# Two adaLN layers on one core: part of the convolution's front moved into the MLP before it

## The chip, the cores and the metric

The kernel runs on one core of a Trainium2 chip. The metric is the time of one execution on the device in microseconds (us). The engines: PE is TensorE (matmuls, and transposes by the identity), DVE is VectorE, ACT is ScalarE, POOL is GpSimd, SP is SyncE, which here only issues DMA.

## The reference

Input x has shape (2, 2048, 128). Layer 0 is a gated linear attention and then two blocks of windowed attention with a gated MLP; layer 1 is a causal convolution by softmaxed scores and a mixture of 16 experts. What matters here is the seam between them:

```python
# end of L0: second block's MLP
x = x + h @ w2 + b2                    # h = a * gelu(g), a, g from layernorm(shift_token(x)) @ w1 + b1
...
x = x + gb * _L0_ffn_ref(...)          # gate and residual of layer 0
# start of L1
h = _layernorm(x, axis=-1) * (1 + ca) + sa
x = x + ga * _L1_attn_ref(h, ...)
# _L1_attn_ref: 16 heads of 8
z = softmax(einsum('bse,he->bsh', x, W_A) * SCALING, axis=1)     # over the 2048 positions
v = einsum('bse,fe->bsf', x, W_V)
out[i] = sum over j <= i of z[i - j] * v[j]                        # per head
return out @ W_O.T + b_O
# then
h = _layernorm(x, axis=-1) * (1 + cb) + sb
x = x + gb * _L1_ffn_ref(h, ...)       # gate, top 2 of 16 experts, relu
```

## The kernel before

The 4096 rows are 32 tiles of 128 rows, 16 per batch element; they stay in SBUF as `x_rows`, and what layer 0's second half makes is in `y_rows`. Four tiles form a group, so there are eight groups. Each stage is a block with one hand-written program per engine; engines meet only through semaphores inside a block, and all of them meet at a barrier between blocks.

**The layers' block** (`layers_in_one_block`, L1436) runs attention, MLP, attention, MLP. The order of an engine's work is set by `Phase` (L164): a list of stages, each a function with a lag, and step s calls every stage for group s minus its lag, in the order of the list. For the MLP (`gated_mlp`, L1238) the lists are: TensorE `up` (lag 2, three gate and three up products), `turn` (1), `down` (3); VectorE `residual` (4, adds the down product to `y_rows`), `statistics` (0), `multiply` (2, three products), `normalize` (0); ScalarE `gelu` (2, three) and `hn_columns` (1); GpSimd `inverse_std` (0). `between` holds calls that are made ahead of a step. A phase of the second MLP has steps 0 to 11.

**The convolution's block** (`convolution_and_experts`, L1850) comes next. Its front is, per group: GpSimd gates y (`gated`, L1951), VectorE adds it to x and takes layer-norm statistics (`statistics`, L1981 to L1991), GpSimd raises to the power of minus a half (`inverse_std`, L1957), VectorE makes offsets (L1996), ScalarE normalizes four tiles into `cv_rows` (`normalized`, L2199), TensorE turns them (`turn_h`, L2092), ScalarE copies the columns to `cv_hT` with scale and shift (`h_columns`, L2207), TensorE projects to scores z (L2100) and values v (L2109), and ScalarE evicts both (`outputs`, L2215 and L2218). VectorE takes a maximum per group (`group_max`, L2002). When a batch element's four groups are in, ScalarE takes the exponential of 16 x 2048 scores (`z_exp`, L2224) and VectorE normalizes them (`probabilities`, L2017). SyncE then writes them to DRAM (L1939) and fetches them back as Toeplitz tiles `cv_toep` (L1932), 32 blocks wide in three parts, for each of eight convolution steps. There is one such buffer: the next step's part is fetched when the matmuls have used it (`p_used`).

Behind the front stands the experts' set-up (`experts`, L1492): ten rounds, in each of which TensorE fills a PSUM bank (`prepare`: rounds 0 to 3 transpose four weight tiles each, 4 and 5 make the gate, 6 to 9 are the first batch element's products) and ScalarE (even rounds) or VectorE (odd rounds) evicts it (`take`, L1736 and L1615). `set_bank` names the bank, and a round waits until the bank's last one has been evicted:

```python
set_bank = lambda r: bk[r % 2 + (2 if r < ROUNDS_BEFORE else 0)]     # L1543
...
set_done(pe, r - 2)                                                   # L1785
```

Then TensorE runs the convolution (`convolve`, L2124), which waits for `vnow` from ScalarE (L2233), with the experts' phases behind and between. GpSimd meanwhile adds the output bias to x (L1970).

## Time and profile before

| | us |
|---|---|
| three runs, median (lowest to highest) | 1212.86 (1210.7 to 1214.95) |
| the profiled execution's own time | 1215.1 |
| its span in the profile | 1213.3 |
| TensorE busy in the span | 1068.4 (88%) |
| VectorE, ScalarE, GpSimd busy | 879.7, 818.5, 661.1 |
| mean granted TensorE clock | 0.955 |

The span is the time from the first to the last instruction in the profile. "Busy" counts the time in which an engine executes something. The granted clock is the share of TensorE's full 2.4 GHz clock; it has two levels, 1.0 and 0.5. Lines named L... are those of the kernel before; the changed kernel has other numbers.

### The profile page before, as it was taken

The page shows a single profiled execution, that of the slowest core. Times are in us where ns is not written, and L with a number is a line of the kernel's source. Part 1 is how long each engine was busy: PE and PEld are TensorE (multiplying, and loading weights), DVE is VectorE, ACT ScalarE, POOL GpSimd, SP SyncE. Part 2 cuts the span into 40 slices and gives each one's busy share as a digit, 9 for nine tenths or more (in the row PEclk, how much of TensorE's full clock was granted, in tenths as well). Part 3 has the DMA queues.
Part 4 walks back from the last instruction along what each step waited for, and adds up shares of the span by engine and source line. Part 5 has one row for each costly group of instructions (what it writes and reads, how often), then busy time and mean ns, then how long its engine had stood idle before and what let it go on. Part 6 is the DMA issues. An engine that isn't in the chain of part 4 may idle for free. (4 is left out here: it accounts for less than half of the span.)

```text
span 1213.3 us, 33822 instructions
## 1 busy us (share of the span) xinstructions
PE 1068.4 (88%) x11683; PEld 733.6 (60%) x11683; DVE 879.7 (73%) x2948; ACT 818.5 (67%) x2658; POOL 661.1 (54%) x1070
## 2 busy tenths in 40 slices
PE   6699994799999998798899999997996778799996
PEld 4467673377777776465577777775663577654442
DVE  4799997588888886374788888885547312079998
ACT  3688883588888887323888988884327403178886
POOL 1578995788888886111888888882106300002222
PEclk9899997799999998989999999998997899899998
DMA  7000000112222121311112111111001486600000
GB/s 232 2 2 11 11 2 1 27 45 55 57 52 54 45 46 45 117 32 34 41 44 47 45 44 45 45 45 27 1 1 44 92 194 137 142 5 16 16 18 18
DMA packets 69566, 58.79 MB, mean 48 GB/s; under 512 B 42262, under 2 KB 53442, under 8 KB 69122
## 3 DMA queue, kind: packets, MB, share of 16 engines
q1 hardware_dynamic: 69411, 56.83, 19.3%
q8 instruction: 84, 1.38, 0.5%
q14 instruction: 71, 0.58, 0.2%
HBM read 29.40 MB, written 2.38 MB: 26 GB/s over the span
## 5 line engine op out<-in xcount | busy, mean ns | idle before, releaser
L1168 PE MATMUL psum<-wa_wqkv,wa_hT 128*128 128x512 f32 x384 | 189.8, 603 | 4.4 <-DVE wa_tmp L1032 3.2
L1124 ACT ACTIVATE wa_p<-psum,wa_nb 128x128 f32<-128x128 f32 x512 | 183.7, 398 | 4.3 <-DVE wa_nb L1048 4.2
L1048 DVE CUSTOM_DVE_ANT_0 psum<-psum,wa_bias 128x128 f32<-128x128 f32 x512 | 133.0, 323 | 51.2 <-PE psum L1197 51.2
L1014 POOL TENSOR_TENSOR wa_p<-wa_p,wa_rrs 128x512 f32<-128x512 f32 x128 | 133.2, 1040 | 47.7 <-DVE wa_rrs L1057 47.7
L1594 POOL TENSOR_TENSOR ex_total<-ex_total,mod 128x128 f32<-128x128 f32 x32 | 15.5, 485 | 218.3 <-DVE ex_total L1722 218.3
L1124 ACT ACTIVATION_READ_ACCUMULATOR wa_p<-psum,wa_nb 128x1 f32 x512 | 122.2, 239 | 0.0
L1840 PE MATMUL psum<-ex_wc,ex_hT 128*128 128x512 f32 x256 | 117.6, 602 | 3.4 <-DVE ex_yw L1705 2.2
L1769 ACT ACTIVATE ex_yw<-psum,ex_w 128x128 f32<-128x128 f32 x384 | 106.7, 400 | 20.1 <-DVE ex_w L1698 7.4
L985 POOL TENSOR_TENSOR wa_qr<-wa_qr,wa_tmp 128x512 f32<-128x512 f32 x64 | 81.8, 1278 | 64.3 <-DVE wa_tmp L1032 64.3
L1134 ACT ACTIVATE wa_pT<-psum 128x512 f32<-128x512 f32 x128 | 76.6, 598 | 39.7 <-PE psum L1177 39.7
L1381 ACT ACTIVATE ml_gelu<-psum,ml_b 128x512 f32<-128x512 f32 (+1 forms) x48 | 32.9, 685 | 85.0 <-PE psum L1408 71.6
L1177 PE MATMUL psum<-ident,wa_p 128*128 128x128 f32 x512 | 81.0, 282 | 9.5 <-ACT wa_kT L1117 3.2
L1032 DVE TENSOR_TENSOR wa_tmp<-psum,wa_tabs 128x512 f32<-128x512 f32 x128 | 87.2, 681 | 0.0
L1168 PEld LDWEIGHTS psum<-wa_wqkv,wa_hT 128*128 128x128 f32 x384 | 64.3, 195 | 37.9 <-issue 32.9
L1840 PEld LDWEIGHTS psum<-ex_wc,ex_hT 128*128 128x128 f32 x256 | 45.2, 189 | 65.8 <-issue 65.0
L990 POOL TENSOR_TENSOR wa_kr<-wa_kr,wa_tmp 128x512 f32<-128x512 f32 x64 | 81.5, 1273 | 2.2 <-DVE wa_tmp L1032 2.2
L2124 PE MATMUL psum<-cv_v_now,cv_toep 64*64 64x256 f32 (+31 forms) x2048 | 67.8, 290 | 15.1 <-DMA cv_toep<-cv_zpad 7.6
L1220 PE MATMUL psum<-wa_wo,wa_oT 128*128 128x128 f32 x512 | 70.8, 283 | 11.1 <-DVE wa_oT L1063 11.1
L1722 DVE TENSOR_TENSOR ex_yw<-ex_yw 128x1024 f32<-128x1024 f32 (+2 forms) x96 | 78.4, 816 | 1.7 <-ACT ex_yw L1769 0.8
L1039 DVE TENSOR_REDUCE wa_ss<-wa_sq 128x16 f32<-128x1024 f32 x64 | 77.4, 1210 | 1.6 <-ACT wa_sq L1095 1.5
L2124 PEld LDWEIGHTS psum<-cv_v_now,cv_toep 64*64 64x64 f32 x2048 | 62.6, 142 | 21.0 <-issue 17.9
L1048 DVE DVE_READ_ACCUMULATOR2_ANT wa_nb<- 128x1 f32 x512 | 72.5, 142 | 0.0
(256 smaller groups left out, 2978.2 us busy)
## 6 DMA issues: line engine op xcount, KB each, us to landing
wa_vm<-wa_v SPq DMA_DIRECT2D x127, 128.0 KB, 2.3
cv_toep<-cv_zpad SPq DMA_DIRECT2D x32, 256.0 KB, 4.5
cv_toep<-cv_zpad SPq DMA_DIRECT2D x16, 512.0 KB, 6.9
wa_tabs<-in_rotations_dram SPq DMA_DIRECT2D x2, 2048.0 KB, 8.2
wa_rows<-y_rows SPq DMA_DIRECT2D x31, 128.0 KB
wa_rows<-y_rows SPq DMA_DIRECT2D x31, 127.0 KB
x_rows<-in_L_attn_x_dram SPq DMA_DIRECT2D x4, 512.0 KB, 6.0
out_dram<-x_rows SPq DMA_DIRECT2D x32, 64.0 KB, 1.5
```

The source lines that it names most:

```text
L985: nc.gpsimd.tensor_tensor(q, q, tmp[:, t % 2, 0, :], ALU.add).then_inc(g_q.sem, 1)
L990: nc.gpsimd.tensor_tensor(k, k, tmp[:, t % 2, 1, :], ALU.add).then_inc(g_k.sem, 1)
L1014: nc.gpsimd.tensor_tensor(p, p, cols_bc(rrs[:, t % 2, r, :], P), ALU.mult)\
L1032: nc.vector.tensor_tensor(halves(heads(cross)), halves(src)[:, :, ::-1, :], halves(rows_bc(sin, WH)), ALU.mult).then_inc(done.sem, 1)
L1048: m = nc.vector.tensor_tensor_reduce(out=s, in0=s, in1=edges, scale=-1.0, scalar=MAX_FLOAT, op0=ALU.add, op1=ALU.min, accum_out=nb[:, t % ...
L1124: e = nc.scalar.activation(pr[:, t % 2, r, h, :], sim_bank[r][:, P * h:P * h + P], ACT.Exp, bias=nb[:, t % 2, r, h:h + 1], scale=-1.0, acc ...
L1168: nc.tensor.matmul(bank, hT[:, t % 3, :], wqkv[:, INNER * k:INNER * k + INNER], start=True, stop=True).then_inc(done.sem, 1)
L1177: m = nc.tensor.transpose(turn_bank[:, P * k:P * k + P], src(t, k), c.ident[:, :])
L1722: nc.vector.tensor_tensor(to, y[:, 0:n, :], y[:, n:2 * n, :], ALU.add).then_inc(v_half[k].sem, 1)
L1769: m = nc.scalar.activation(yw[:, t % 2, e, :], up_banks[(4 * t + k) % 6][:, P * j:P * j + P], ACT.Relu, scale=w[:, t // GT % 2, t % GT, e: ...
L1840: nc.tensor.matmul(up_banks[number % 6], hT[:, t // GT % 3, t % GT, :], wc[:, batch(t), chunk(k)], start=True, stop=True).then_inc(p_up[k] ...
L2124: mm = nc.tensor.matmul(conv_bank[a][side(k), CD * lag:CD * BLOCKS] .rearrange("p (n d) -> p n d", d=CD), toep[side(a), k, HALF * lag:HALF ...
```

## The change

- A class `ConvolutionRows` holds the front's tiles and its functions `gated`, `statistics`, `inverse_std`, `offsets`, `normalized`, and the turning of the convolution's weights. Its constant `IN_MLP` is 5.
- In the second MLP these functions run for groups 0 to 4, each in its engine's phase with a lag of 5 (4 for the gate). The weights are loaded by SyncE behind its staging, turned by TensorE after the last down projection, and copied by ScalarE after a table load.
- In the convolution's block only groups 5 to 7 remain. GpSimd gates all three, then takes the three powers; VectorE does all statistics, then all offsets, then the weights and the mixing matrix, and only then the maxima. ScalarE normalizes into `y_rows` in place of a ring `cv_rows`, and does not wait for the turn before it.
- ScalarE's first exponential stands behind the outputs of group 3, where it stood behind those of group 5.
- The ten set-up rounds go over six banks in place of two.
- A group's four `bn_aggr` no longer have a wait and a no-op before each.

```diff
+class ConvolutionRows:
+    IN_MLP = TILES // 4 - 3
...
+    def gated(self, gp, g):
+        c, t = self.c, self.tiles(self.y, g)
+        b = 4 * g // NT
+        c.nc.gpsimd.tensor_tensor(t, t, rows_bc(c.mod[:, 0, b, GB, :], 4), ALU.mult).then_inc(self.g_gated.sem, 1)
...
+    def statistics(self, dve, g):
+        nc, x = self.c.nc, self.c.x
+        self.g_gated.wait(dve, g)
+        t = self.tiles(x, g)
+        nc.vector.tensor_tensor(t, t, self.tiles(self.y, g), ALU.add).then_inc(self.v_x.sem, 1)
...
+    def normalized(self, act, g):
+        self.v_shift.wait(act, g)
+        for t in range(4 * g, 4 * g + 4):
+            m = self.c.nc.scalar.activation(self.y[:, t, :], self.c.x[:, t, :], ACT.Identity,
+                                            scale=self.rstd[:, t:t + 1], bias=self.shift[:, t:t + 1])
+        m.then_inc(self.a_norm.sem, 1)
...
+        def conv_rows(eng, do, lag):
+            def f(g):
+                if g - first < conv.IN_MLP:
+                    do(eng, g - first)
+            return [] if more else [(f, lag)]
...
-            return Phase([(inverse_std, 0)], first, GROUPS)
+            return Phase(conv_rows(gp, conv.inverse_std, 5) + [(inverse_std, 0)] +
+                         ([] if more else [(conv_gated, 4)]), first, GROUPS)
...
-            return Phase([(residual, 4), (statistics, 0), (multiply, 2), (normalize, 0)], first, GROUPS,
+            return Phase([(residual, 4)] + conv_rows(dve, conv.statistics, 5) +
+                         [(statistics, 0), (multiply, 2), (normalize, 0)] + conv_rows(dve, conv.offsets, 5), first, GROUPS,
...
+            if not more:
+                between[10] = lambda: nc.scalar.preload_act_table_set("natural_log_exp_and_others")
+                between[11] = lambda: conv.copy_weights(act, turn_bank)
+            return Phase([(gelu, 2), (hn_columns, 1)] + conv_rows(act, conv.normalized, 5), first, GROUPS,
...
+            return Phase([(up, 2), (turn, 1), (down, 3)], first, GROUPS, begin=lambda: wait_layer(pe, l),
+                         between=None if more else {11: conv_weights})
...
-    set_bank = lambda r: bk[r % 2 + (2 if r < ROUNDS_BEFORE else 0)]
+    set_bank = lambda r: bk[2 + (r + 4) % 6 if r < ROUNDS_BEFORE else r % 2]
+    SET_BANKS = 6
...
-                set_done(pe, r - 2)
+                set_done(pe, r - (SET_BANKS if r < ROUNDS_BEFORE else 2))
...
-                for g in range(GROUPS + 2):
-                    if g < GROUPS:
-                        normalized(g)
+                for g in range(1, GROUPS + 2):
+                    if conv.IN_MLP <= g + 1 < GROUPS:
+                        conv.normalized(act, g + 1)
...
-                    if g == PER_B + 3:
+                    if g == PER_B + 1:
                         z_exp(0)
```

VectorE in a middle step of the second MLP, before (names that begin with ml_ are the MLP's, with wa_ the attention's, with cv_ the convolution's):

```order
L1355 TENSOR_TENSOR y_rows<-y_rows,psum 128x512 [waits ml_p_down]
L1327 BN_STATS ml_st<-wa_rows 128x6 [waits wa_rows_in3] x4
L1331 BN_AGGR ml_mv<-ml_st 128x2 [waits ml_v_bn_mv]
L1348 SCALAR_TENSOR_TENSOR ml_mT<-psum,ml_b,ml_gelu 128x512 [waits ml_p_up,ml_a_gelu,ml_p_down]
L1348 SCALAR_TENSOR_TENSOR ml_mT<-psum,ml_b,ml_gelu 128x512 [waits ml_p_up,ml_a_gelu]
L1348 SCALAR_TENSOR_TENSOR ml_mT<-psum,ml_b,ml_gelu 85x512 [waits ml_p_up,ml_a_gelu]
L1338 TENSOR_SCALAR ml_hn<-wa_rows,ml_mv,ml_rstd 128x128 [waits ml_p_hn,ml_g_eps_rstd]
```

and the same step in the changed kernel:

```order
L1460 TENSOR_TENSOR y_rows<-y_rows,psum 128x512 [waits ml_p_down]
L1300 TENSOR_TENSOR x_rows<-x_rows,y_rows 128x512 [waits cv_g_gated]
L1303 BN_STATS cv_st<-x_rows 128x6 [waits cv_v_x_stat]
L1307 BN_AGGR cv_mv<-cv_st 128x2 [waits cv_v_x_stat]
L1311 TENSOR_SCALAR cv_mv<-cv_mv 128x4 [waits cv_v_x_stat]
L1432 BN_STATS ml_st<-wa_rows 128x6 [waits wa_rows_in3] x4
L1436 BN_AGGR ml_mv<-ml_st 128x2 [waits ml_v_bn_mv]
L1453 SCALAR_TENSOR_TENSOR ml_mT<-psum,ml_b,ml_gelu 128x512 [waits ml_p_up,ml_a_gelu,ml_p_down]
L1453 SCALAR_TENSOR_TENSOR ml_mT<-psum,ml_b,ml_gelu 128x512 [waits ml_p_up,ml_a_gelu]
L1453 SCALAR_TENSOR_TENSOR ml_mT<-psum,ml_b,ml_gelu 85x512 [waits ml_p_up,ml_a_gelu]
L1443 TENSOR_SCALAR ml_hn<-wa_rows,ml_mv,ml_rstd 128x128 [waits ml_p_hn,ml_g_eps_rstd]
L1316 SCALAR_TENSOR_TENSOR cv_shift<-cv_mv,cv_rstd 128x4 [waits cv_g_rstd]
```

Four operations came in ahead of the MLP's own statistics, and the offset behind its normalization.

ScalarE in the front of the convolution's block, changed kernel, around the first exponential (L1323 is `normalized`, L2261 `h_columns`, L2269 and L2272 `outputs`, L2278 `z_exp`):

```order
L2261 ACTIVATE cv_hT<-psum,mod_cols 128x512 [waits cv_p_v,cv_p_h]
L2269 ACTIVATE cv_z<-psum 16x512 [waits cv_p_z]
L2272 ACTIVATE cv_v<-psum 128x512 [waits cv_p_v]
L2278 ACTIVATE cv_z,cv_zsum<-cv_z,cv_zneg 16x2048 [waits cv_v_zneg]
L1323 ACTIVATE y_rows<-x_rows,cv_shift,cv_rstd 128x128 [waits cv_v_shift]
L1323 ACTIVATE y_rows<-x_rows,cv_shift,cv_rstd 128x128 x3
L2261 ACTIVATE cv_hT<-psum,mod_cols 128x512 [waits cv_p_v,cv_p_h]
```

Here the exponential stands between the outputs of group 3 and the normalized rows of group 7; before, it stood behind the last normalized rows and the outputs of group 5, with the columns of group 7 after it.

TensorE in the experts' set-up, before and then changed:

```order
L1789 MATMUL psum<-ident,ex_w_in 128x128 [waits ex_loaded,cv_a_v]
L1789 MATMUL psum<-ident,ex_w_in 128x128 x7
L1789 MATMUL psum<-ident,ex_w_in 128x128 [waits ex_a_set]
L1789 MATMUL psum<-ident,ex_w_in 128x128 x3
L1789 MATMUL psum<-ident,ex_w_in 128x128 [waits ex_v_set]
L1791 MATMUL psum<-ident,ex_gate_in 128x16 [waits ex_a_set]
L1796 MATMUL psum<-ex_gateT,ex_mix 128x16 [waits ex_a_set,ex_v_mix,ex_v_set]
```

```order
L1905 MATMUL psum<-ident,ex_w_in 128x128 [waits ex_loaded,cv_a_v]
L1905 MATMUL psum<-ident,ex_w_in 128x128 x15
L1907 MATMUL psum<-ident,ex_gate_in 128x16
L1912 MATMUL psum<-ex_gateT,ex_mix 128x16 [waits ex_a_set,ex_v_mix]
L1916 MATMUL psum<-ex_wT,ex_mix 128x512 [waits ex_a_set]
```

The sixteen transposes and the gate's transpose wait for no eviction of a set-up bank any more.

## Rows read from the trace of the kernel before

**Rows 1.** Stages: busy us (count) per engine, granted clock, DMA share, GB/s
```profile
855.29:908.42 53.13, 52.25 (x262) 33.55 (x260) 26.78 (x73) 16.22 (x23) 5.00 (x8) 1.00 0.00 1
909.42:948.61 39.19, 24.82 (x307) 14.26 (x307) 27.40 (x103) 29.69 (x63) 20.19 (x19) 0.83 0.16 38
948.61:963.53 14.92, 9.28 (x29) 4.99 (x30) 8.15 (x15) 5.15 (x10) 10.80 (x8) 0.77 0.61 141
963.53:1060.00 96.47, 79.28 (x2229) 72.91 (x2230) 14.11 (x51) 17.15 (x44) 0.00 (x0) 0.93 0.68 154
```

**Rows 2.** Timeline, TensorE, second MLP: start, us, line, operation, [idle before <-releaser]
```profile
863.56 1.02 PE L1408 MATMUL psum<-ml_hnT,ml_w 128*128 128x512 f32 x2
...
871.83 1.02 PE L1408 MATMUL psum<-ml_hnT,ml_w 128*128 128x512 f32 x2
```

**Rows 3.** Timeline, VectorE, end of that MLP step
```profile
868.98 0.75 DVE L1348 SCALAR_TENSOR_TENSOR ml_mT<-psum,ml_b,ml_gelu 85x512 f32<-85x512 f32 x1 [0.97 <-PE psum L1412]
869.65 1.10 DVE L1338 TENSOR_SCALAR ml_hn<-wa_rows,ml_mv,ml_rstd 128x128 f32<-128x128 f32 x4
```

**Rows 4.** Timeline, ScalarE, first GELU of the next step
```profile
872.89 0.69 ACT L1381 ACTIVATE ml_gelu<-psum,ml_b 128x512 f32<-128x512 f32 x1 [2.76 <-PE psum L1408]
```

**Rows 5.** Timeline, VectorE, front of the convolution's block and second softmax
```profile
910.87 1.74 DVE L1981 TENSOR_TENSOR x_rows<-x_rows,y_rows 128x512 f32<-128x512 f32 x1 [1.73 <-POOL y_rows L1951]
912.65 0.87 DVE L1984 BATCH_NORM_STATS2 cv_st<-x_rows 128x6 f32<-128x128 f32 x4
913.44 0.37 DVE L1988 BATCH_NORM_AGGREGATE cv_mv<-cv_st 128x2 f32<-128x6 f32 x4
...
916.63 0.15 DVE L1996 SCALAR_TENSOR_TENSOR cv_shift<-cv_mv,cv_rstd 128x4 f32<-128x4 f32 x1
916.73 0.69 DVE L1981 TENSOR_TENSOR x_rows<-x_rows,y_rows 128x512 f32<-128x512 f32 x1
...
944.80 1.27 DVE L2017 TENSOR_SCALAR cv_z<-cv_z,cv_zrec 16x2048 f32<-16x2048 f32 x1
946.00 1.26 DVE L2002 TENSOR_REDUCE cv_zpart<-cv_z 16x1 f32<-16x512 f32 x2
...
952.09 2.05 DVE L2017 TENSOR_SCALAR cv_z<-cv_z,cv_zrec 16x2048 f32<-16x2048 f32 x1
```

**Rows 6.** Timeline, GpSimd, first two gates and the bias additions
```profile
909.59 2.47 POOL L1951 TENSOR_TENSOR y_rows<-y_rows,mod 128x512 f32<-128x512 f32 x2
...
949.35 10.80 POOL L1970 TENSOR_TENSOR x_rows<-x_rows,cv_bog 128x512 f32<-128x512 f32 x8 [12.81 <-DVE cv_bog L2025]
```

**Rows 7.** Timeline, ScalarE, front of the convolution's block and set-up
```profile
916.82 1.65 ACT L2199 ACTIVATE cv_rows<-x_rows,cv_shift,cv_rstd 128x128 f32<-128x128 f32 x4 [3.64 <-DVE cv_shift L1996]
...
921.20 0.76 ACT L2207 ACTIVATE cv_hT<-psum,mod_cols 128x512 f32<-128x512 f32 x1
...
948.61 2.01 ACT L2224 ACTIVATE cv_z<-cv_z,cv_zneg 16x2048 f32<-16x2048 f32 x1
...
950.61 0.57 ACT L1736 ACTIVATE ex_wT<-psum 128x512 f32<-128x512 f32 x1
```

**Rows 8.** Timeline, TensorE, front of the convolution's block and set-up
```profile
912.02 0.33 PE L2153 MATMUL psum<-ident,cv_w_in 128*128 128x128 f32 x1 [3.61 <-DMA cv_w_in<-in_L_attn_W_A_dram]
...
918.52 1.11 PE L2092 MATMUL psum<-ident,cv_rows 128*128 128x128 f32 x4 [5.90 <-ACT cv_rows L2199]
...
924.22 1.98 PE L2109 MATMUL psum<-cv_wvT,cv_hT 128*64 128x64 f32 x32
...
930.60 1.15 PE L2109 MATMUL psum<-cv_wvT,cv_hT 128*64 128x64 f32 x32
...
954.80 1.12 PE L1789 MATMUL psum<-ident,ex_w_in 128*128 128x128 f32 x4 [2.91 <-DVE ex_wT L1615]
...
957.57 5.32 PE L1800 MATMUL psum<-ex_wT,ex_mix 128*128 128x512 f32 x8
```

**Rows 9.** Window of one us, TensorE busy, granted clock, DMA share, GB/s
```profile
912.00:913.00 1.00, 0.60 (x3) 0.86 0.28 55
```

More of the change, by code:

```diff
@@ L1240, in gated_mlp @@
+def gated_mlp(c, y, given, ctx, conv):
     nc, inp, bk = c.nc, c.inp, c.bank
@@ L1306, in sync @@
                     given.stage(sp, "attention", l + 1, GT * g, GT)
+            else:
+                conv.load(sp)
         def gpsimd(gp):
@@ L1317, in inverse_std, with conv_gated @@
                   .then_inc(g_rstd.sem, 1)
-            return Phase([(inverse_std, 0)], first, GROUPS)
+            def conv_gated(g):
+                v_y.wait(gp, g)
+                if g - first < conv.IN_MLP:
+                    conv.gated(gp, g - first)
+            return Phase(conv_rows(gp, conv.inverse_std, 5) + [(inverse_std, 0)] +
+                         ([] if more else [(conv_gated, 4)]), first, GROUPS)
         def vector(dve):
@@ L1424, in down, with conv_weights @@
                 m.then_inc(p_down.sem, 1)
-            return Phase([(up, 2), (turn, 1), (down, 3)], first, GROUPS, begin=lambda: wait_layer(pe, l))
+            def conv_weights():
+                a_hn.wait(pe, last)
+                conv.turn_weights(pe, turn_bank)
+            return Phase([(up, 2), (turn, 1), (down, 3)], first, GROUPS, begin=lambda: wait_layer(pe, l),
+                         between=None if more else {11: conv_weights})
         readers = {turn_at: a_hn, down_at: v_y}
@@ L1947, in _ @@
                 nc.gpsimd.memset(zeros[:, :], 0.0).then_inc(g_zero, 1)
-                def gated(g):
-                    t = tiles_of(y, g)
-                    nc.gpsimd.tensor_tensor(t, t, rows_bc(c.mod[:, 0, batch(g), GB, :], GT), ALU.mult)\
-                      .then_inc(g_gated, 1)
-                def inverse_std(g):
-                    gp.wait_ge(v_eps, g + 1)
-                    t = slice(GT * g, GT * g + GT)
-                    nc.gpsimd.tensor_tensor(rstd[:, t], mv[:, t, 1], c.minus_half[:, 0:GT], ALU.pow)\
-                      .then_inc(g_rstd, 1)
-                for g in range(GROUPS + 1):
-                    if g < GROUPS:
-                        gated(g)
-                    if g >= 1:
-                        inverse_std(g - 1)
+                late = range(conv.IN_MLP, GROUPS)
+                for g in late:
+                    conv.gated(gp, g)
+                for g in late:
+                    conv.inverse_std(gp, g)
                 on_gpsimd.fill(gp)
@@ L1967, in _ @@
                 for g in range(GROUPS):
-                    gp.wait_ge(a_norm, GT * g + GT)
+                    conv.a_norm.wait(gp, g)
                     t = tiles_of(c.x, g)
@@ L2042, in _ @@
                 dve.sem_inc(v_conv, 1)
-                for g in range(GROUPS + 4):
-                    if g < GROUPS:
-                        statistics(g)
-                    if 1 <= g <= GROUPS:
-                        offsets(g - 1)
-                    if g >= 4:
-                        group_max(g - 4)
-                    if g == PER_B + 4:
-                        probabilities(0)
+                late = range(conv.IN_MLP, GROUPS)
+                for g in late:
+                    conv.statistics(dve, g)
+                for g in late:
+                    conv.offsets(dve, g)
                 weights()
                 on_vector.mixing(dve)
+                for g in range(GROUPS):
+                    group_max(g)
+                    if g == PER_B - 1:
+                        probabilities(0)
                 probabilities(1)
@@ L2192, in _ @@
             def _(act):
-                def normalized(g):
-                    act.wait_ge(v_shift, g + 1)
-                    if g >= 2:
-                        act.wait_ge(p_h, g - 1)
-                    for i in range(GT * g, GT * g + GT):
-                        nc.scalar.activation(rows[:, g % 2, i % GT, :], c.x[:, i, :], ACT.Identity,
-                                             scale=rstd[:, i:i + 1], bias=shift[:, i:i + 1]).then_inc(a_norm, 1)
                 def h_columns(g):
```

138 lines of the change are left out of this document (75 added, 63 removed).

## The prediction

> **What bounds the kernel now.** I read the busy times by stage first, because a share over the whole span hides which stage pays [rows 1]. The second MLP (855.29 to 908.42 us) has TensorE busy for 52.25 of 53.13 us at full clock, with VectorE at 26.78, ScalarE at 16.22 and GpSimd at 5.00: TensorE bounds it, and the others have room. The next stage, the convolution's front (909.42 to 948.61), has no full engine: TensorE 24.82 of 39.19, ScalarE 29.69, at a mean clock of 0.83. A chain is the bound there. Then come 14.92 us from the last value eviction to the convolution's first matmul (TensorE 9.28, clock 0.77), and eight convolution steps that take 96.47 us, or 12.1 us each. The change touches the first three. The rest should only start earlier.
>
> Next the timelines of the engines. One MLP step on TensorE starts at 863.56 and the next at 871.83, so a step is 8.27 us [rows 2]. VectorE does its last multiplication, which waits for TensorE, at 868.98, and its normalization at 869.65 to 870.75; it then has nothing to do until the next step's residual some 1.3 us later [rows 3]. ScalarE idles for 2.76 us before it starts the next GELU at 872.89 [rows 4]. In the front stage TensorE's first transposed rows come only at 918.52, having waited for ScalarE's normalized rows, which begin at 916.82 behind GpSimd and VectorE [rows 5 to 8].
>
> **The change, part by part.** *Five groups inside the MLP.* Each adds on VectorE an addition (0.7, as a residual), 0.87 + 0.37 for statistics, and two small operations of 0.15 = 2.25 us [rows 5]. A full MLP step holds the normalization's 1.10, three multiplications of 0.75, a residual of 0.7 and statistics of 1.2, or 5.3 us; the stage's mean is less (26.78 us in 6.4 steps, 4.2), since its last steps lack parts. 5.3 + 2.25 = 7.6 of 8.27: it fits. The new work stands ahead of the multiplications, which pushes the first two back by 2.1 us; the third waited for TensorE anyway (0.97 us) and stays where it is. GpSimd gets a gate of 1.25 [rows 6] and a power on top of the pair it has (5.00 us for four pairs, 1.25 each): at most 3.7 of 8.27. Its order is power of the convolution, power of the MLP, gate, so the gate runs when VectorE starts to normalize. What then happens the trace shows: the addition at 910.87, beside a gate, took 1.74 us where it takes 0.69 alone [rows 5]. I charge up to 1.25 us of such waiting a step. It falls on VectorE's idle 1.3 us at the step's end, which the displaced multiplications leave alone. ScalarE then does four normalized tiles in 1.65 us [rows 7], from about 871.5 to 873.2, in front of a GELU that would start at 872.89: 0.3 us late, and that GELU's product is wanted by a multiplication 2.1 us later than before. Cost to TensorE, which sets the end: nothing. If the cover goes, every us over 8.27 is paid five times. The weight loads (four DMAs) move to SyncE's queue behind its staging, over 50 us before their use: nothing. Their three transposes and three copies come behind the last down projection and move the end of the block by some 0.4 us (transposes 0.4, copies 0.6, beside a residual of 0.69 that stood there). The table load of 1.3 us falls into ScalarE's idle end.
>
> The Trainium skill ("SBUF — State Buffer", Who interferes with whom) says that the port pair which VectorE and GpSimd share is held exclusively for a whole instruction, by operations with two SBUF inputs or in a two-port mode. By it bn_stats pays nothing and the MLP step stays under 8.27 us, as in the sum; the 1.74 us agrees.
>
> *The front stage, 39.2 us before.* I follow the new order from about 909.9, where the block now starts.
> 1. TensorE turns group 0 at once, where it waited until 918.52 [rows 8]. At full clock a group costs it 24.82 x 0.83 / 8 = 2.6 us by its busy time and mean clock [rows 1]; I take 2.5, as some of that was set-up.
> 2. The three late groups: gate to 911.3, then VectorE's addition waits for the second gate as before (912.5), 3 x 2.1 us of statistics to 919.0, offset, and ScalarE normalizes group 5 at 919.1 to 920.8. ScalarE has that ahead of group 3's columns, so TensorE, done with groups 0 to 2 at 918.9, waits 3 us.
> 3. VectorE goes on with offsets to 920.3, weights 0.85, mixing some 3 us (it took the 2.7 between the first bias addition at 949.35 and the softmax at 952.09, and meets those additions again, 1.35 each [rows 5, 6]), four maxima of 0.63 and two small ones [rows 5], with starts and signals between: 927.3.
> 4. ScalarE has the first exponential, 2.0 us, at that point of its order, then normalization of group 7 (1.65) and columns of group 5 (0.76) [rows 7]: 931.6. TensorE has stood since about 928: over 4 us.
> 5. Three groups of 2.5 us and their evictions: 939.4 at full clock.
> That gives a stage end of 939.4 against 948.61, 9.2 us less. But TensorE's granted clock dropped to half (mean 0.86 in the slice) in the us after it had idled from 908.42 to 912.02 [rows 8, 9], and the same 32 matmuls took 1.98 us at half and 1.15 at full clock [rows 8]. The wait of step 4 is as long. Half clock over some 4.4 us of three groups' work costs 2.1 us. I take that: the stage ends at 941.5, **7.1 us less**. Bounds: 9.2 with no fall, and 5 if the clock stays low through the three groups.
>
> The Trainium skill ("TensorE: Matmul & The Clock Gate", HAM oscillation) warns against just such gaps between bursts; a kernel that obeyed it would be worth 9.2 here, and it gets 7.1. The row agrees that a gap of this size can do it.
>
> *From the last eviction to the convolution, 14.9 us before.* TensorE waited in the set-up for one bank after another, the worst time 2.91 us for VectorE's copy, which stood behind the second softmax; then its last eight passes took 5.32 us at mostly half clock [rows 8]. With six banks the sixteen transposes need no eviction. ScalarE: exponential 2.0, two copies of 0.57 [rows 7], a small one, so the gate round comes at +3.2 us. VectorE's normalization of the second softmax no longer meets the bias additions (the 2.05 at 952.09 become the 1.27 of 944.80 [rows 5]), and its copies of 0.7 come from +3.5 on, in time. Four rounds of 0.93 (the MLP's pairs of passes, six in the 5.2 us ahead of its down projection, take 0.86 each) bring TensorE to +7.1, the last copy to +7.8. 14.9 - 7.8 = **7.1 us less**. Bounds: 8 with nothing late, 4 if the rounds run at half clock.
>
> *Earlier softmax.* VectorE's result was ready at 946.07 [rows 5], and store and first fetch were in place by 963.53 at the latest, where TensorE started without a transfer to wait for: at most 17.5 us. Now it is ready at about 931.1, so all is in place by 948.6 at the latest, and the convolution starts at 949.3. Worth nothing by itself, needed so that nothing is lost. GpSimd's eight bias additions move from 949 to 921 on and are waited for by nobody then. Eight convolution steps depend on one Toeplitz buffer each, not on a clock on the wall: they move as they are.
>
> Sum: -7.1 - 7.1 = -14.2 us, with the late block end in it. The profiled execution has 1215.1 us for a span of 1213.3; the median of three is 1212.86, 2.2 less, and I take the difference from the median: **1198.7 us**.
>
> **The rivals.** *Clock stays full* through the softmax wait: -16.3, 1196.6. For it: a gap may be shorter than I draw. Against: 3.61 us were enough [rows 8, 9]. *Clock low for longer*, also after the wait of step 2 or in the set-up: 2 to 4 us more, 1200.7 to 1202.7. *VectorE becomes the MLP's bound*: its 7.6 us plus more waiting for GpSimd than its tail covers (the addition, the small addition after the statistics and the normalization, up to 1.25 each, make 7.6 + 2.5 = 10.1). 1 to 1.8 us over in five steps gives back 5 to 9 us: 1203.7 to 1207.7. For it: the 1.74 row. Against: GpSimd's operations start after the VectorE ones they wait for, so only one of three can meet. *Slower:* the same ring closes over ScalarE: GELU waits behind the normalized tiles, those for the offset, that for the power, that for the statistics, and the multiplication for GELU. It decides from a step of 8.27 + 14.2/5 = 11.1 us on; at 12 us the time is 1212.9 - 14.2 + 5 x 3.7 = 1217.2. Against it are the 2.76 us that ScalarE idles before each GELU [rows 4]. *The change does not do what it says:* the front gets shorter, but the convolution's steps, with DMA at 0.68 [rows 1] and waits for transfers, meet the clock at other points and give a good part back: 1206 to 1213.
>
> **How the numbers follow.** Forecast (1197.5 to 1200.5) 0.50; full clock 0.17; low clock longer 0.12; MLP bound by VectorE 0.11; gains given back 0.06, half of it within the limit; slower 0.04. The range 1195.0 to 1204.5 takes in the forecast, the clock cases, their unknown waits and the mild end of the MLP case, some 0.83. A measurement here tells about 0.3% (3.6 us) from no change: faster 0.93, same 0.03, slower 0.04.
>
> **What would show it.** Steps of 8.27 us still in the second MLP; the block change at about 909.9; transposed rows right behind it; ScalarE idle before the first exponential, which begins near 927; TensorE idle for about 4 us behind group 4 and at half clock after; the last value eviction near 941.5; the set-up's wait for VectorE gone and the first convolution matmul near 949.3; from there to the end the same time as before. Wrong would be an MLP step above 8.5 us, a first convolution matmul that waits for a transfer, or a convolution of more than 98 us.

## The result, and the profile after

| kernel | median, us | runs | lowest to highest | ratio to the kernel before (95%) |
|---|---|---|---|---|
| before, beside it | 1214.95 | 7 | 1210.70 to 1219.01 | 1 |
| with the change | 1200.61 | 7 | 1197.35 to 1207.50 | 0.9885 (0.9856 to 0.9915) |

The change takes 14.3 us off (1214.95 less 1200.61), or 1.15%. The profiled execution of the changed kernel has 1197.35 us for a span of 1195.5, the fastest of its seven. That of before has 1215.1 for 1213.3.

The stages of the changed kernel, in busy times: the MLP up to its last down projection, the front up to the last value eviction, the set-up of the mixing, and the eight convolution steps. They answer to [rows 1]; each column is a sum over the engine, with its number of instructions, and then the mean granted clock.

```profile
core 0: us, PE busy (x) PEld busy (x) DVE busy (x) ACT busy (x) POOL busy (x), PEclk, DMA share, GB/s
856.73:909.86 53.13, 52.26 (x264) 33.72 (x262) 38.08 (x128) 25.30 (x44) 16.28 (x18) 1.00 0.00 1
911.15:942.59 31.44, 24.06 (x304) 14.13 (x304) 19.81 (x55) 21.37 (x39) 18.14 (x17) 0.89 0.34 82
942.59:950.79 8.20, 6.25 (x30) 3.78 (x30) 4.10 (x7) 4.91 (x9) 0.00 (x0) 1.00 0.48 100
950.79:1041.23 90.44, 72.86 (x2209) 67.74 (x2210) 13.16 (x48) 16.78 (x43) 0.00 (x0) 1.00 0.72 165
```

The MLP takes 53.13 us as before, although VectorE now works 38.08 us in it (26.78 before) and GpSimd 16.28 (5.00). The front went from 39.19 to 31.44 us and the set-up from 14.92 to 8.20. The block starts 1.29 us behind the last down projection (911.15 less 909.86), where it was 1.00. That is -7.75 - 6.72 + 0.29 = **-14.2 us**, the forecast's sum.

The two profiled spans differ by more, 17.8 us, and this is what the other stages add. The second MLP starts 1.4 us later in this execution (856.73 against 855.29); what stands before it is the same in both kernels. The eight convolution steps take 90.44 us against 95.42 (963.53 to 1058.95; the last window of [rows 1] runs 1.05 us past them): the clock was full through all of them (1.00 above). A second profile of the same changed kernel, below, gives 95.92 at 0.93. So those 5 us are the luck of one execution, and the medians' 14.3 is the number to keep. It agrees with the 14.2 of the stages.

Now the MLP's steps in detail. TensorE's down projections, one group to a line (the start, the duration, engine, line, operation, tiles, shapes and count):

```profile
862.31 2.84 PE L1532 MATMUL psum<-ml_w,ml_mT 128*128 128x128 f32 x24
870.58 2.84 PE L1532 MATMUL psum<-ml_w,ml_mT 128*128 128x128 f32 x24
878.85 2.84 PE L1532 MATMUL psum<-ml_w,ml_mT 128*128 128x128 f32 x24
```

They stand 8.27 us apart, as in [rows 2]. VectorE's timeline of that step, with the idle time before an operation and what ended it in brackets, GpSimd's beside it, and ScalarE's two rows at its end:

```profile
865.19 0.69 DVE L1460 TENSOR_TENSOR y_rows<-y_rows,psum 128x512 f32<-128x512 f32 x1 [1.27 <-PE psum L1532]
...
869.11 2.05 DVE L1453 SCALAR_TENSOR_TENSOR ml_mT<-psum,ml_b,ml_gelu 128x512 f32<-128x512 f32 x3
871.08 1.64 DVE L1443 TENSOR_SCALAR ml_hn<-wa_rows,ml_mv,ml_rstd 128x128 f32<-128x128 f32 x4
872.65 0.15 DVE L1316 SCALAR_TENSOR_TENSOR cv_shift<-cv_mv,cv_rstd 128x4 f32<-128x4 f32 x1
873.46 0.69 DVE L1460 TENSOR_TENSOR y_rows<-y_rows,psum 128x512 f32<-128x512 f32 x1 [0.67 <-PE psum L1532]
```
```profile
869.59 1.03 POOL L1415 TENSOR_TENSOR ml_rstd<-ml_mv,minus_half 128x4 f32<-128x4 f32 x1
870.60 1.26 POOL L1288 TENSOR_TENSOR y_rows<-y_rows,mod 128x512 f32<-128x512 f32 x1
```
```profile
872.83 1.65 ACT L1323 ACTIVATE y_rows<-x_rows,cv_shift,cv_rstd 128x128 f32<-128x128 f32 x4 [1.27 <-DVE cv_shift L1316]
874.38 0.67 ACT L1487 ACTIVATE ml_gelu<-psum,ml_b 128x512 f32<-128x512 f32 x1
```

VectorE's step is 873.46 - 865.19 = 8.27 us, and 0.67 us of it are still idle. The normalization takes 1.64 us instead of 1.10 [rows 3], since GpSimd's gate runs at 870.60 to 871.86. ScalarE's GELU has lost the idle time of [rows 4] to the normalized tiles and comes directly behind them. Its place in the step has hardly moved: it starts 0.92 us behind the residual (874.38 less 873.46), where it was 0.86 (872.89 less the residual at 872.03 in the trace of before).

The front on TensorE, from its first transposed rows on (this answers to [rows 8]):

```profile
911.19 1.06 PE L2159 MATMUL psum<-ident,y_rows 128*128 128x128 f32 x8 [0.96 <-PEq L1583]
...
919.99 0.66 PE L2159 MATMUL psum<-ident,y_rows 128*128 128x128 f32 x4
924.38 1.86 PE L2167 MATMUL psum<-cv_hT,cv_waT 128*16 128x512 f32 x2 [3.73 <-ACT cv_z L2269]
926.18 1.78 PE L2176 MATMUL psum<-cv_wvT,cv_hT 128*64 128x64 f32 x32
...
933.70 1.18 PE L2167 MATMUL psum<-cv_hT,cv_waT 128*16 128x512 f32 x2 [2.52 <-ACT cv_z L2269]
934.80 1.98 PE L2176 MATMUL psum<-cv_wvT,cv_hT 128*64 128x64 f32 x32
```

There are **two** waits, and the granted clock falls after each. The first, 3.73 us, stands ahead of group 3's projection: ScalarE copies group 3's columns only after it has normalized group 5. The second, 2.52 us, stands ahead of group 5's projection, behind the first exponential. At half clock the two score matmuls behind the first wait take 1.86 us where they take 1.03 at full clock, and the 32 value matmuls behind the two waits take 1.78 and 1.98 instead of 1.15. The first wait begins here, on GpSimd and VectorE (this answers to [rows 5, 6]):

```profile
911.32 3.72 POOL L1288 TENSOR_TENSOR y_rows<-y_rows,mod 128x512 f32<-128x512 f32 x3
```
```profile
912.61 2.98 DVE L1300 TENSOR_TENSOR x_rows<-x_rows,y_rows 128x512 f32<-128x512 f32 x1 [2.04 <-POOL y_rows L1288]
```

VectorE's first addition is issued when the first gate is done and ends 0.55 us after the third is (915.59 and 915.04): 2.98 us for an operation of 0.69. Group 5 is then normalized at 921.45 (ScalarE), 10.3 us behind the block's start.

The set-up, which in [rows 8] waited for one bank after another:

```profile
942.64 1.97 PE L1905 MATMUL psum<-ident,ex_w_in 128*128 128x128 f32 x16 [0.70 <-ACT cv_v L2272]
...
945.84 0.59 PE L1912 MATMUL psum<-ex_gateT,ex_mix 128*128 128x16 f32 x4 [1.07 <-ACT ex_gateT L1852]
946.27 3.68 PE L1916 MATMUL psum<-ex_wT,ex_mix 128*128 128x512 f32 x8
950.79 1.49 PE L2191 MATMUL psum<-cv_v_now,cv_toep 64*64 64x256 f32 x24 [0.83 <-ACT cv_v_now L2287]
```

All sixteen transposes run in one piece, the last eight passes are at full clock (3.68 us for 5.32 before), and the convolution starts without a transfer to wait for.

### The profile page after: what moved, and what is told of

The parts are those of the page before. It is cut to its first block and busy times, and to the rows that moved or that the text cites. A ratio compares the mean times of both kernels' runs of the same rounds, so it can differ in the third digit from the quotient of the medians.

```text
span 1195.5 us, 33784 instructions
## 1 busy us (share of the span) xinstructions
PE 1059.4 (89%) x11683; PEld 728.9 (61%) x11683; DVE 879.8 (74%) x2948; ACT 820.7 (69%) x2658; POOL 659.8 (55%) x1070
## 3 DMA queue, kind: packets, MB, share of 16 engines
q8 instruction: 84, 1.38, 0.5%
## 5 line engine op out<-in xcount | busy, mean ns | idle before, releaser
L1177 PE MATMUL psum<-ident,wa_p 128*128 128x128 f32 x512 | 80.8, 281 | 10.1 <-ACT wa_kT L1117 3.2
L2191 PE MATMUL psum<-cv_v_now,cv_toep 64*64 64x256 f32 (+31 forms) x2048 | 63.9, 279 | 15.4 <-DMA cv_toep<-cv_zpad 7.9
L1220 PEld LDWEIGHTS psum<-wa_wo,wa_oT 128*128 128x128 f32 x512 | 64.9, 199 | 12.1 <-DVE wa_oT L1063 12.1
```

What stands on the lines that cost most here:

```text
L1177: m = nc.tensor.transpose(turn_bank[:, P * k:P * k + P], src(t, k), c.ident[:, :])
L1220: m = nc.tensor.matmul(hw_bank[:, 0:E], oT[:, t % 2, k, :], wo[:, k, :], start=k == 0, stop=k == PAIRS - 1)
```

## The experiments

Theory A is the forecast's: the front and the banks each give about 7 us, the early exponential gives nothing but keeps the transfers ahead, and the waits in the front cost a fall of the clock. The rivals say that one part carries the whole gain, that the early exponential costs time, or that VectorE in the MLP is near its limit. Twelve kernels were run in three sets, each set beside its own runs of the kernel before (medians 1216.96, 1216.85 and 1215.79). The ratio of *triple_stats* rests on two runs, the others on four to ten. The stages below are from one profiled execution each, in us. "Delay" is from the last down projection's end to the block's first instruction. The last column is the sum of the three to its left, the one to compare, since it leaves out what happened upstream and in the convolution. Among the variants of the changed kernel the intervals of the ratios overlap, so most differences between them are shown by the stages alone; that the stages repeat, *after_again* shows.

| kernel | median | ratio (95%) | delay | front | set-up | sum |
|---|---|---|---|---|---|---|
| before | 1214.95 | 1 | 1.00 | 39.19 | 14.92 | 55.1 |
| changed | 1200.61 | 0.9885 (0.9856 to 0.9915) | 1.29 | 31.44 | 8.20 | 40.9 |
| two_banks | 1204.59 | 0.9904 (0.9874 to 0.9934) | 1.30 | 31.50 | 14.16 | 47.0 |
| late_softmax | 1197.72 | 0.9851 (0.9811 to 0.9890) | 1.29 | 29.11 | 8.43 | 38.8 |
| mlp_alone | 1205.73 | 0.9904 (0.9871 to 0.9937) | 1.30 | 29.11 | 13.78 | 44.2 |
| six_alone | 1209.23 | 0.9960 (0.9936 to 0.9984) | 1.00 | 39.22 | 9.93 | 50.2 |
| fill | 1200.10 | 0.9869 (0.9831 to 0.9908) | 1.30 | 29.97 | 8.20 | 39.5 |
| gates | 1201.07 | 0.9863 (0.9845 to 0.9882) | 1.21 | 29.04 | 8.20 | 38.5 |
| in6 | 1198.64 | 0.9852 (0.9828 to 0.9875) | 2.68 | 28.10 | 8.19 | 39.0 |
| triple_stats | 1203.32 | 0.9882 (0.9860 to 0.9904) | 1.30 | 31.45 | 8.20 | 41.0 |
| after_again | 1200.97 | 0.9870 (0.9836 to 0.9905) | 1.30 | 31.44 | 8.20 | 40.9 |
| best1 | 1194.92 | 0.9831 (0.9799 to 0.9863) | 3.73 | 25.39 | 8.43 | 37.6 |
| conv_fill | 1202.03 | 0.9886 (0.9859 to 0.9914) | 1.30 | 31.44 | 8.21 | 41.0 |
| best1_fill | 1198.85 | 0.9857 (0.9828 to 0.9886) | 3.74 | 26.25 | 8.43 | 38.4 |

**The parts of the change, undone or alone.** *two_banks* is the changed kernel with its set-up on two banks:

```diff
-    set_bank = lambda r: bk[2 + (r + 4) % 6 if r < ROUNDS_BEFORE else r % 2]
-    SET_BANKS = 6
+    set_bank = lambda r: bk[r % 2 + (2 if r < ROUNDS_BEFORE else 0)]
+    SET_BANKS = 2
```

> The changed kernel with the experts' set-up on two banks again. Theory (the gain is two separate parts, front and set-up): the front from block start to last value eviction keeps its 31 us; the stretch from there to the first convolution matmul goes back from 8.2 us to 13 to 15, with TensorE again idle before its third and fourth transposing rounds; the time is 5 to 7 us over the changed kernel, some 1206. Rival (the banks gave nothing, the set-up only gained because the bias additions and the mixing matrix had left VectorE): the stretch stays near 9 us and the time near 1201.

The set-up takes 14.16 us instead of 8.20; nothing else moves. TensorE's timeline in it:

```profile
937.04 1.09 PE L1905 MATMUL psum<-ident,ex_w_in 128*128 128x128 f32 x8 [0.70 <-ACT cv_v L2272]
939.61 1.12 PE L1905 MATMUL psum<-ident,ex_w_in 128*128 128x128 f32 x4 [1.47 <-ACT ex_wT L1852]
...
944.00 6.53 PE L1916 MATMUL psum<-ex_wT,ex_mix 128*128 128x512 f32 x8
```

The wait for ScalarE's copy is 1.47 us and two shorter ones for VectorE's copies follow, 0.5 and 0.6, where the changed kernel has one of 1.07. The clock falls in these waits, to a mean of 0.56 over the last eight passes, which take 6.53 us instead of 3.68. **The six banks are worth 6.0 us here**, about half of it (2.85) in those passes. The median is 12.4 us under its own kernel before, where the changed one is 14.3 under: a smaller loss than the stages' 6.1, but the intervals of the two ratios overlap.

*late_softmax* puts the first exponential back behind group 7's normalized tiles:

```diff
-                    if g == PER_B + 1:
+                    if g == PER_B + 3:
                         z_exp(0)
```

> The changed kernel with the first exponential behind the outputs of group 5 again. Theory (its early place only keeps the Toeplitz fetch out of the way and costs TensorE a wait): TensorE's wait ahead of group 5's projection goes, the front is 1 to 3 us shorter, the first fetch ends near 953 and the convolution's first matmul still waits for no transfer; the time is 0 to 3 us under the changed kernel's. Rival (the early softmax is what lets the convolution start): the first convolution matmuls wait for the transfer, 3 us or more over the changed kernel.

The first matmul of the convolution waits for ScalarE's copy of the values, as in the changed kernel, and for no transfer; the first step runs in one piece:

```profile
946.22 8.07 PE L2191 MATMUL psum<-cv_v_now,cv_toep 64*64 64x256 f32 x256 [0.83 <-ACT cv_v_now L2287]
```

The front is 2.3 us *shorter* with the exponential late (29.11 against 31.44) and the set-up 0.2 longer. The eight convolution steps take 95.12 us, no longer than in the second profile of the changed kernel. So the early softmax protects nothing and costs 2.1 us by the stages (the intervals of the two ratios overlap): the two microseconds of exponential stand in front of group 7's normalized tiles in ScalarE's order, and TensorE's 2.52 us of waiting with its fall come from them.

*mlp_alone* has both edits. What is left of the change is the five groups in the MLP and what came with them: the weights that are loaded and turned in the MLP's block, where TensorE had waited 3.61 us for them [rows 8], the new order of the late groups' operations, and the `bn_aggr` without their waits.

> The changed kernel with both undone: two banks, late exponential; only the five groups in the MLP remain. Theory: front 29 to 32 us in place of 39.2, MLP steps 8.27 us, set-up stretch 13 to 15 us; 7 to 9 us under the kernel before, some 1206. Rival (moved rows only gain where the rest of the change uses them): under 4 us.

The front is 29.11 us: **the move is worth 10.1 us there by itself**, less the 0.3 of delay; the set-up gains 1.1 more. The median is 11.2 us under its kernel before, more than the 7 to 9 expected. No run splits the move into its groups, its weights and its order. *six_alone* is the kernel before with six banks and nothing else:

```diff
-    set_bank = lambda r: bk[r % 2 + (2 if r < ROUNDS_BEFORE else 0)]
+    set_bank = lambda r: bk[2 + (r + 4) % 6 if r < ROUNDS_BEFORE else r % 2]
...
-                set_done(pe, r - 2)
+                set_done(pe, r - (6 if r < ROUNDS_BEFORE else 2))
```

> The kernel before with the set-up rounds on six banks and nothing else. Theory: the stretch from the last value eviction to the first convolution matmul is bound by VectorE's copies, which stand behind mixing matrix and second softmax until about 954, so it shrinks from 14.9 to 10 to 12 us; 3 to 5 us under the kernel before, some 1211. Rival (banks alone give the full 6.7 us seen in the changed kernel): 1208. Second rival (nothing): 14.9 us remain.

The set-up goes from 14.92 to 9.93, 5.0 us, and the front doesn't move (39.22). One part after the other, by the table's sums: the kernel before 55.1, with the move 44.2 (-10.9), with the banks besides 38.8 (-5.4), with the early exponential as well 40.9 (+2.1), which is the changed kernel. The banks give 5.0 to 6.1 us whatever else is there, so neither gain leans on the other.

**What the clock costs in the front.** *fill* lets TensorE turn the identity 24 times ahead of the score matmuls of groups 3 and 5, where it had stood idle, into a bank that is free there; the output is the same:

```diff
+                    if g in (PER_B, PER_B + 2):
+                        for n in range(24):
+                            nc.tensor.transpose(bk[0][:, P * (n % 4):P * (n % 4) + P], c.ident[:, :], c.ident[:, :])
                     if g >= 1:
                         project(g - 1)
```

> The changed kernel with 24 transposes of the identity, 2.6 us of TensorE work into a bank that nobody reads, ahead of group 3's and of group 5's projection, where TensorE stood idle for 3.73 and 2.52 us. Theory (the waits cost twice, as waits and by the half clock that follows them, 924 to 928 and 934 to 938): no half clock in the front, and the last value eviction 1.5 to 3 us earlier after the block's start, 28.5 to 30 us in place of 31.4. Rival (the front is bound by VectorE and ScalarE, so TensorE's clock in it is free): 31 to 31.5 us, or more where the filling ends behind the wait.

```profile
914.91 2.78 PE L2224 MATMUL psum<-ident 128*128 128x128 f32 x24
918.81 1.02 PE L2167 MATMUL psum<-cv_hT,cv_waT 128*16 128x512 f32 x2 [1.12 <-ACT cv_z L2272]
...
924.49 2.78 PE L2224 MATMUL psum<-ident 128*128 128x128 f32 x24
928.12 1.02 PE L2167 MATMUL psum<-cv_hT,cv_waT 128*16 128x512 f32 x2 [0.85 <-ACT cv_z L2272]
```

TensorE's waits turn into transposes and the score matmuls behind them are at full clock (1.02). TensorE still waits 1.12 and 0.85 us behind them, so they delay nothing themselves. The front is 29.97 us: the two falls together cost 1.5 us, less than the 2.1 that the forecast charged for one, since TensorE still has waits for VectorE and ScalarE to take the rest up. The median of four runs (1193.9 to 1205.1) doesn't tell the kernel from the changed one.

**Where the front waits.** *gates* leaves only the last group's gate behind the MLP; the other seven are issued in its steps:

```diff
-                if g - first < conv.IN_MLP:
+                if g - first < GROUPS - 1:
                     conv.gated(gp, g - first)
...
-                for g in late:
-                    conv.gated(gp, g)
+                conv.gated(gp, GROUPS - 1)
```

> The changed kernel with the gates of groups 5 and 6 also in the MLP's last steps, where GpSimd is idle; the convolution's block starts with one gate in place of three. Theory (TensorE's first wait of 3.7 us comes from VectorE's addition, 2.98 us behind GpSimd's gates, and from the three statistics ahead of the first offset): the addition takes 0.7 to 1.7 us, starts 1.4 us earlier, and group 5 is normalized some 3 us earlier; the first wait shrinks to about 1 us with no half clock after it; the front takes 28 to 30 us. Rival (the softmax sets the front, as forecast): 31 us remain, since the first exponential waits for VectorE's maxima.

```profile
911.90 1.84 DVE L1300 TENSOR_TENSOR x_rows<-x_rows,y_rows 128x512 f32<-128x512 f32 x1 [0.62 <-PEq L1583]
```
```profile
922.53 1.02 PE L2166 MATMUL psum<-cv_hT,cv_waT 128*16 128x512 f32 x2 [1.26 <-ACT cv_z L2268]
...
931.85 1.87 PE L2166 MATMUL psum<-cv_hT,cv_waT 128*16 128x512 f32 x2 [3.47 <-ACT cv_z L2268]
```

The addition starts 0.13 us behind the block's start (911.77), where it was 1.46, and takes 1.84 us instead of 2.98; the first wait falls from 3.73 to 1.26 us with no fall of the clock behind it. The whole front gives 2.4 us, and the wait at the exponential grows to 3.47: the limit moves to the next place. The median of 1201.07 us shows nothing of the 2.4.

*in6* puts one group more into the MLP:

```diff
-    IN_MLP = TILES // 4 - 3
+    IN_MLP = TILES // 4 - 2
```

> The changed kernel with six groups in the MLP. Theory (the MLP's last steps still have room): the MLP's last down projections keep their 3.72 us, the block starts 1 to 1.5 us later, since group 5's offset and normalized rows come beside the last residual; the front shrinks from 31.4 to 27 to 29 us; 1 to 3 us under the changed kernel. Rival (five was the most that fits): what the front gains the block's start loses, and more; the changed kernel's time or above.

The front is 28.10, but the block starts 2.68 us behind the last down projection. Of 3.34 us gained 1.4 are given back, and 1.95 stay.

**Is VectorE near its limit in the MLP?** *triple_stats* takes the convolution's statistics of a group three times in the MLP, into scratch, with the output unchanged:

```diff
-        self.st6, self.mv = sb("cv_st6", [P, 4, 6]), sb("cv_mv", [P, TILES, 2])
+        self.st6, self.mv = sb("cv_st6", [P, 12, 6]), sb("cv_mv", [P, TILES, 2])
...
+        for i in range(8 if g < self.IN_MLP else 0):
+            m = nc.vector.bn_stats(self.st6[:, 4 + i, :], x[:, 4 * g + i % 4, :])
```

> The changed kernel with eight more statistics instructions in each of the five moved groups (1.7 us of VectorE work whose result nobody reads). It measures how much cover the MLP step has. VectorE idled 0.67 us in the full steps. Theory (the cover ends there): a step goes from 8.27 to 9.2 to 9.4 us where the MLP's own statistics and normalization are still in it, three steps, and stays 8.27 in the last ones: 3 us longer in all. Rival (the displaced multiplications have slack of a whole step, so that nothing is paid): 8.27 everywhere.

VectorE's residuals, then TensorE's down projections:

```profile
866.28 0.69 DVE L1462 TENSOR_TENSOR y_rows<-y_rows,psum 128x512 f32<-128x512 f32 x1 [1.28 <-PE psum L1534]
875.35 0.68 DVE L1462 TENSOR_TENSOR y_rows<-y_rows,psum 128x512 f32<-128x512 f32 x1
884.41 0.68 DVE L1462 TENSOR_TENSOR y_rows<-y_rows,psum 128x512 f32<-128x512 f32 x1
```
```profile
863.40 2.84 PE L1534 MATMUL psum<-ml_w,ml_mT 128*128 128x128 f32 x24
871.66 2.84 PE L1534 MATMUL psum<-ml_w,ml_mT 128*128 128x128 f32 x24
```

VectorE's steps are 9.07 us long, 0.8 over TensorE's, and TensorE keeps its 8.27. My theory expected that each step over 8.27 would be paid; it fell. VectorE may trail: there are three such steps, after which its residual starts 5.26 us behind the down projection's start instead of 2.88, so it is 2.4 us late, and the last steps, which lack the next group's statistics and normalization, take that up. How far it could trail before TensorE paid, no run shows. The delay, the front and the set-up are those of the changed kernel to 0.1 us.

**Together.** *after_again* is the changed kernel in the set of the last three.

> The changed kernel itself, once more, beside the next three. Both theories: block start to last value eviction 31.4 us, set-up 8.2 us, MLP steps 8.27 us, as in its first profile, since nothing in them depends on chance; the convolution's eight steps anywhere from 90 to 97 us, by how often TensorE's clock falls in them; time 1198 to 1203.

Its stages repeat to 0.01 us, but the convolution's steps take 95.92 us at 0.93:

```profile
947.25:1043.17 95.92, 78.39 (x2209) 72.22 (x2210) 13.16 (x48) 16.77 (x43) 0.00 (x0) 0.93 0.69 155
```

TensorE's waits for the Toeplitz transfers come to the same sum in both profiles (7.9 us in six waits, 8.0 in five), but the single waits differ. In after_again the two longest are 2.19 and 2.30 us, and the part behind them, 2.49 us at full clock, is slow:

```profile
964.08 3.56 PE L2191 MATMUL psum<-cv_v_now,cv_toep 64*64 64x128 f32 x128 [2.19 <-DMA cv_toep<-cv_zpad]
1019.19 4.02 PE L2191 MATMUL psum<-cv_v_now,cv_toep 64*64 64x128 f32 x128 [2.30 <-DMA cv_toep<-cv_zpad]
```

At the same two places the first profile has waits of 1.79 and 1.63 us and keeps the full clock. A third fall of after_again comes between the fourth and the fifth step, behind waits of 0.89 and 1.38 us, where the first profile has the same two and no fall. So a long wait is not the whole cause; six_alone waits 2.61 us for a transfer and fill 2.24, too, and both keep the clock there.

*best1* has the edits of in6, late_softmax and gates.

> Six groups in the MLP, the gates of all but the last group there too, and the first exponential behind the outputs of group 5. Theory (what is left of the front is two waits, one made by the gates and late statistics, one by the exponential's place): TensorE goes through the eight groups with no wait above 1 us, the front takes 24 to 27 us, the block starts 1.4 us later behind the last down projection; 4 to 6 us under the changed kernel. Rival (the chain only moves: VectorE's maxima or the ScalarE queue hold the front at 28 us): 1 to 3 us under it.

```profile
914.41 1.61 PE L2158 MATMUL psum<-ident,y_rows 128*128 128x128 f32 x8 [3.40 <-PEq L1583]
916.04 1.89 PE L2166 MATMUL psum<-cv_hT,cv_waT 128*16 128x512 f32 x2
...
937.02 1.02 PE L2166 MATMUL psum<-cv_hT,cv_waT 128*16 128x512 f32 x2 [1.27 <-ACT cv_z L2268]
```

From the block's start on TensorE never waits over 1.27 us and the front is 25.39, but the block starts 3.73 us behind the last down projection (2.4 later than in the changed kernel, where 1.4 was expected), after 3.40 us of idle TensorE, and the clock is low for the first group. VectorE and ScalarE show what holds it:

```profile
910.82 1.22 DVE L1316 SCALAR_TENSOR_TENSOR cv_shift<-cv_mv,cv_rstd 128x4 f32<-128x4 f32 x1 [1.12 <-POOL cv_rstd L1293]
911.96 0.67 DVE L1460 TENSOR_TENSOR y_rows<-y_rows,psum 128x512 f32<-128x512 f32 x1
```
```profile
912.07 1.65 ACT L1323 ACTIVATE y_rows<-x_rows,cv_shift,cv_rstd 128x128 f32<-128x128 f32 x4 [4.00 <-DVE cv_shift L1316]
```

The sixth group's small operation (0.15 us alone) waits for GpSimd's power and then takes 1.22 us beside its gate, and ScalarE's normalized tiles and copies end the block behind it. The sum is still 3.4 us under the changed kernel's, and the median of six runs, 1194.92 us, is 6 us below after_again's of the same set. The intervals of the two ratios overlap (0.9799 to 0.9863, 0.9836 to 0.9905), so the order of the two is likely rather than settled; against the kernel before it is 1.7% faster.

*conv_fill* is the changed kernel with twelve turned identities in each convolution step ahead of a wait for its transfer, *best1_fill* the same on best1:

```diff
+                        if r == 2:
+                            for n in range(12):
+                                nc.tensor.transpose(bk[2][:, P * (n % 4):P * (n % 4) + P], c.ident[:, :], c.ident[:, :])
                         pe.wait_ge(toep_in[r], (s + 1) * (16 * SIDES))
```

> The changed kernel with twelve transposes of the identity (1.3 us at full clock, into a bank that nobody reads) ahead of each convolution step's third part, where TensorE waits for a transfer. Theory (the spread between profiles of one kernel, and the part of the gain that was seen behind the convolution's start, is TensorE's clock falling in those waits): the eight steps take 90 to 92 us with no half clock in them, the runs lie within 3 us of each other, and the median is 2 to 4 us under the changed kernel. Rival (the clock falls by other gaps too, between the steps): steps of 93 to 97 us and half clock in the convolution remain.

> The two kernels before this one put together. Theory: their gains add, since one lies ahead of the convolution and the other inside it; front 24 to 27 us, convolution 90 to 92 us, 6 to 9 us under the changed kernel, some 1193. Rival: no more than the better of the two.

```profile
950.76 5.54 PE L2194 MATMUL psum<-cv_v_now,cv_toep 64*64 64x256 f32 x128 [0.84 <-ACT cv_v_now L2290]
956.23 1.53 PE L2188 MATMUL psum<-ident 128*128 128x128 f32 x12
```
```profile
950.76:1045.97 95.21, 84.90 (x2305) 1.00 0.68 157
1045.97:1060.00 14.03, 12.65 (x130) 0.76 0.00 1
```

The clock stays full through the eight steps (1.00), and they still take 95.21 us, not the 90 to 92 expected. Each step pays 1.53 us for transposes, also the first ones, which have no transfer to wait for: 12.2 us of filling in eight steps against 7.9 us of waits in the first profile of the changed kernel. What this adds is about what the falls cost over the stage. A fall then comes behind the steps (0.76 from 1045.97 on). The runs lie closer together (1201.5 to 1205.4 against 1193.5 to 1202.6), and nothing is gained. On best1 it costs 3.9 us (1198.85 less 1194.92).

## Why the prediction was right

The forecast was 1198.7 us in 1195.0 to 1204.5; measured were 1200.61. The kernel before had 1214.95 in the same set instead of the 1212.86 that the forecast started from, so by differences it is -14.2 forecast and -14.3 measured. Some of that closeness is errors that cancel.

1. **The MLP's cover.** Right: steps of 8.27 us, and a block 0.3 us later (0.4 forecast). The charge of 1.25 us a step for meeting GpSimd was 0.5 (1.64 less 1.10). Wrong was "if the cover goes, every us over 8.27 is paid five times": triple_stats put VectorE 0.8 us over in three steps, the full ones, and nothing was paid. The rival built on it (1203.7 to 1207.7) had a price that was too high.
2. **The front.** The stage was forecast 31.6 us long (909.9 to 941.5) and took 31.44. Two steps of the path were off. Step 2 had the addition get in behind the second gate, "as before"; with three gates in a row it got in behind the third, and group 5 was normalized 10.3 us after the start, not 9.2. TensorE's wait there was 3.73 us, not 3, and dropped the clock, so there were two falls where the forecast had one. Step 4 had TensorE wait over 4 us for the exponential, though its own times give 3.6 (928 to 931.6); it began at 928.78 with TensorE delayed by step 2's wait, and 2.52 us were left. Both waits together were 6.25 us against 6.6 to 7 forecast, and the clock cost 1.5 us for two falls instead of 2.1 for one (fill).
3. **The set-up.** 8.20 us against 7.8. The price of the banks by themselves is 6.0 (two_banks) or 5.0 (six_alone).
4. **"Worth nothing by itself, needed so that nothing is lost."** Wrong on both counts. late_softmax lost nothing in the convolution and won 2.3 us in the front. I had counted the exponential's 2.0 us in step 4 as part of the path without asking what the front would be without it there. The MLP move's own worth in the front, 10.1 us, was hidden behind that in my -7.1.
5. **The convolution's steps.** They move as they are: 95.42 before, and 95.92 and 90.44 in two profiles of the changed kernel, each time without a transfer to wait for at the first matmul. From the last step's matmul to the end both kernels take 154.3 us. The rival in which gains are given back there didn't happen. What I called "12.1 each" (96.47 / 8, with the 1.05 us too many) is a number with about 5 us of luck in eight.

The Trainium skill ("TensorE: Matmul & The Clock Gate", HAM oscillation) warns of idle gaps between bursts. This case's rows show falls behind waits of 3.73 and 2.52 us, and show as well what the warning doesn't: taking the falls away gave 1.5 us in the front, which is bound by a chain, and nothing in the convolution, where the filling cost more than the waits that it replaced (12.2 us against 7.9).

Still open: by how much best1 is better than the changed kernel, why the single transfer waits of the convolution differ from execution to execution, and why the clock falls behind some waits and not behind others of the same length. That wasn't tried further.

## What to carry to other kernels

When work moves under an engine that bounds a loop, look for the chain by which its operations wait for each other rather than for the sum of busy times: here an engine trailed the one that bounds the loop by 2.4 us at no cost, since the last steps were lighter. Price each part of a change on the kernel without the other parts; one that looks like a safeguard (the early softmax) may only cost. Where operations of GpSimd stand back to back, move all but one of them away from the VectorE addition that needs them, and expect the gain to be met by the next wait in the chain. Fill a wait to hold the clock only where the filling doesn't outlast the wait.

## What the runs showed of the hardware

- A VectorE addition with two inputs doesn't get in between GpSimd's consecutive gates of 1.24 us: 1.74 us with one gate left (before, and in6), 1.84 beside one (gates), 2.98 with two left, for an operation of 0.69. I had expected a wait for one. The small operation at 910.82 in best1 took 1.22 us in place of 0.15 in the same way.
- TensorE's granted clock went from 2.4 to 1.2 GHz after waits of 3.73 and 2.52 us in the front, and not after 1.26 (gates); before the change it did after 3.61 [rows 8, 9]. A wait of such length isn't needed: in two_banks it fell behind one of 1.47. Nor is it enough: in the convolution the part behind a transfer wait of 2.02 to 2.61 us ran slow in some places and at full clock in others (full after the 2.61 of six_alone). Two profiles of one kernel, whose waits for transfers in the convolution have the same sum, had mean clocks of 1.00 and 0.93 there, 5.5 us apart. The spread of that kernel's runs is larger (1193.5 to 1202.6 for after_again).
- Work put into waits to hold the clock costs what it takes wherever the wait is shorter than the work: 12 transposes, 1.53 us together, in each of eight steps used up all that the full clock gave.
